# Spline chunks as single steps in the PSUM ring, and a new table of step offsets, in a transformer block of 16 sequences

## The reference

```python
x = x + _L0_attn_ref(_layernorm(x, axis=-1), L0_attn_wq, L0_attn_wk, L0_attn_wv, L0_attn_wo)
x = x + _L0_ffn_ref(_layernorm(x, axis=-1), L0_ffn_gate_cp, L0_ffn_up_cp, L0_ffn_down_cp)
# attention: 16 heads of 16; scores q.k / 4, masked where j - i > 16; softmax; times v; times wo.T
# ffn: the three weights are Catmull-Rom splines through about 2033 control points each:
gate_w = spline_reconstruct(gate_cp, INTER, HIDDEN)     # 1024 x 256
up_w = spline_reconstruct(up_cp, INTER, HIDDEN)
down_w = spline_reconstruct(down_cp, HIDDEN, INTER)     # 256 x 1024
inter = jax.nn.silu(gate) * up
return jnp.einsum('bsi,hi->bsh', inter, down_w)
```

## Time and profile before

| what | value |
|---|---|
| median of 3 runs | 655.34 us (653.92 to 655.53) |
| the profiled execution | 653.66 us |
| its span | 651.9 us |
| TensorE busy | 611.8 us (94%), 5568 matmul records |
| VectorE busy | 481.1 us (74%) |
| ScalarE, GpSimd busy | 267.9 us (41%), 200.5 us (31%) |

### The profile page before, as it was taken

One profiled execution on the slowest core, in us unless ns is written; L12 is line 12 of the kernel. 1 busy time (PEld: TensorE's weight loads), 2 busy tenths in 40 slices (PEclk: granted clock), 3 DMA queues, 4 the chain that ended last, 5 costly groups with the idle time before them and its releaser, 6 DMA issues.

```text
span 651.9 us, 14038 instructions
## 1 busy us (share of the span) xinstructions
PE 611.8 (94%) x5568; PEld 527.4 (81%) x5568; DVE 481.1 (74%) x935; ACT 267.9 (41%) x432; POOL 200.5 (31%) x244
## 2 busy tenths in 40 slices
PE   1878989999999999999999999999999999998977
PEld 0455547989889888989888988889898989887977
DVE  6776647876877888787879797878878796863442
ACT  2230345452444445354444345444534444444412
POOL 1540232332233232323332333323232332333313
PEclk9986779999999999999999999999999999998989
DMA  8133030302122322213040312222221303010000
GB/s 229 44 130 113 10 123 6 113 18 98 37 69 62 98 66 69 81 46 102 9 127 14 107 42 82 66 82 67 71 79 33 115 2 116 17 35 1 18 18 17
DMA packets 44113, 42.86 MB, mean 66 GB/s; under 512 B 4528, under 2 KB 42512, under 8 KB 44048
## 3 DMA queue, kind: packets, MB, share of 16 engines
q1 hardware_dynamic: 44048, 41.96, 20.7%
HBM read 12.32 MB, written 4.19 MB: 25 GB/s over the span
## 4 chain that ended last, share of the span: by engine, by line
PE 77%; DVE 19%; issue 2%; POOL 1%; ACT 0%; DVEq 0%; ACTq 0%; POOLq 0%
PE ring L605 13%; PE ring L606 11%; PE ring L607 11%; PE ring L689 6%; PE pair L657 6%; PE ring L612 5%; DVE M L547 5%; PE ring L614 5%; PE ring L613 5%; PE ring L596 4%; PE pair L681 3%; DVE Z L526 3%; PE pair L633 3%; DVE pair L541 2%; PE ring L696 2%
## 5 line engine op out<-in xcount | busy, mean ns | idle before, releaser
L605 PE MATMUL ring<-YT,WGUh 128*128 128x256 f32 x512 | 153.4, 300 | 0.1
L547 DVE TENSOR_REDUCE M<-pair 128x2 f32<-128x288 f32 (+1 forms) x256 | 134.7, 570 | 15.4 <-PE pair L666 11.7
L606 PE MATMUL ring<-YT,WGUh 128*128 128x256 f32 x512 | 144.9, 283 | 0.0
L607 PE MATMUL ring<-YT,WGUl 128*128 128x256 f32 x512 | 144.5, 282 | 0.0
L452 ACT ACTIVATE P<-pair 128x800 f32<-128x800 f32 x128 | 107.1, 838 | 87.5 <-PE pair L681 87.4
L410 POOL TENSOR_TENSOR IN<-GU,IN 128x512 fp32r<-128x512 f32 x64 | 82.2, 1284 | 161.0 <-ACT IN L415 161.0
L605 PEld LDWEIGHTS ring<-YT,WGUh 128*128 128x128 f32 x512 | 97.1, 190 | 6.8 <-issue 3.6
L606 PEld LDWEIGHTS ring<-YT,WGUh 128*128 128x128 f32 x512 | 97.3, 190 | 0.0
L607 PEld LDWEIGHTS ring<-YT,WGUl 128*128 128x128 f32 x512 | 96.9, 189 | 0.0
L402 POOL TENSOR_SCALAR_AFFINE_SELECT P<-P 128x448 f32<-128x448 f32 x64 | 37.6, 588 | 172.7 <-ACT P L452 172.7
L577 DVE SCALAR_TENSOR_TENSOR GU<-GU,ring 128x512 f32<-128x512 f32 x64 | 44.0, 688 | 61.1 <-ACT GU L473 61.0
(11 more groups left out here) (79 smaller groups left out, 1115.1 us busy)
## 6 DMA issues: line engine op xcount, KB each, us to landing
QM<-QK SPq DMA_DIRECT2D x96, 128.0 KB, 2.1
KS<-QK SPq DMA_DIRECT2D x96, 128.0 KB, 2.1
X<-x SPq DMA_DIRECT2D x32, 256.0 KB, 2.9
out<-X SPq DMA_DIRECT2D x16, 256.0 KB, 2.2
OVER<-over SPq DMA_DIRECT2D x4, 256.0 KB, 9.1
TAP<-points SPq DMA_DIRECT2D x4, 192.0 KB, 7.3
POWER<-powers SPq DMA_DIRECT2D x4, 192.0 KB, 7.6
P<-wqk SPq DMA_DIRECT2D x1, 512.0 KB, 5.5
```

The source lines that it names most:

```text
L547: i = nc.vector.tensor_reduce(out=M[:, t % 2, it, :].rearrange("p (a k) -> p a k", a=2)[:, :, n], in_=pr[:, :, cols], axis=AX.X, op=ALU.ma ...
L605: mm(o, wh[:, kb, c], act[:, 0, kb, :], start=j == 0 and kb == 0, stop=False, skip_group_check=True)
L606: mm(o, wh[:, kb, c], act[:, 1, kb, :], start=False, stop=False, skip_group_check=True)
L607: i = mm(o, wl[:, kb, c], act[:, 0, kb, :], start=False, stop=False, skip_group_check=True)
```

## The change

The chunk is no longer done in pairs. It becomes two steps, `wj` (part 0) and `ws` (part 1), each one matmul with a bank of its own in the ring of four; `s1` and `sc` have the two pairs of banks to themselves. VectorE multiplies after `wj` and adds after `ws`. The quarters of the weights are made in the order 0, 2, 1, 3 (`PIECES`), in which `ga` and `up` use them. Waits are cut into pieces: `qk`, `v` and `wo` wait for their own `raw_low`; `ga` and `up` of n = 0, 1 for four chunks in place of eight; `dn` for ten, then twelve. Two guards are added for memory that is used again (`tapped` before the first tanh, `ws_sum` before the first `ic`), and `OVER` and `POWER` change places in memory. All offsets and `PERIOD` are new; turn 3 gets a table of its own.

```diff
+PIECES = (0, 2, 1, 3)
-PERIOD = 33.072
+PERIOD = 33.644
-START = [("raw", 0, 1, 1, -101.93, 0), ("split", 0, 1, 1, -96.87, 0), ("tap", 0, 4, 1, -38.33, 3.572),
+START = [("split", 0, 1, 1, -659.307, 0), ("raw", 0, 1, 1, -233.876, 0), ("tap", 0, 4, 1, -227.012, 29.8767),
...
-RING = ("zt", "qk", "v", "mt", "av", "ot", "on", "wo", "z2", "ga", "up", "dn")
-PAIRS = ("s1", "sc", "ws")
+RING = ("wj", "ws", "zt", "qk", "v", "mt", "av", "ot", "on", "wo", "z2", "ga", "up", "dn")
+PAIRS = ("s1", "sc")
...
-            free[b] = at["y", t, 0] if what == "dn" else k
+            free[b] = at["y", t, 0] if what == "dn" else at["ws", t, n] if what == "wj" else k
...
+                    if t == 0 and n == 0:
+                        act.wait_ge(tapped, len(PIECES))
...
+                    if t == 0 and n == 0:
+                        act.wait_ge(ws_sum, CHUNKS)
...
-                    dve.wait_ge(ws_made, n + 1)
+                    dve.wait_ge(wj_made, n + 1)
                     if n >= 4:
                         dve.wait_ge(ws_low, n - 3)
-                    w, pr = shaped(W[:, n % 4, :], n), pair(what, t, n)
-                    tt(w, shaped(pr[:, 0, :], n), spline_over(n), ALU.mult).then_inc(ws_over, 1)
+                    w = shaped(W[:, n % 4, :], n)
+                    tt(w, shaped(bank("wj", t, n)[:], n), spline_over(n), ALU.mult).then_inc(ws_over, 1)
+                    dve.wait_ge(ws_made, n + 1)
                     dve.wait_ge(ws_over, n + 1)
-                    tt(w, w, shaped(pr[:, 1, :], n), ALU.add).then_inc(ws_sum, 1)
+                    tt(w, w, shaped(bank(what, t, n)[:], n), ALU.add).then_inc(ws_sum, 1)
...
-                elif what == "ws" and (n % 2 or n >= 8):
+                elif what in ("wj", "ws"):
+                    m, j = chunk(n)
+                    part = ("wj", "ws").index(what)
                     pe.wait_ge(rows_loaded, DMA)
...
+                    pe.wait_ge(tapped, PIECES.index(j) + 1)
+                    mm(bk[:], ROWS[32 * m:32 * m + 32, part, :], TAP[32 * m:32 * m + 32, j * 512:(j + 1) * 512],
+                       start=True, stop=True).then_inc((wj_made, ws_made)[part], 1)
...
-                    pe.wait_ge(raw_low, 3)
+                    pe.wait_ge(raw_low, 1)
...
-                    pe.wait_ge(ws_low, 8)
+                    pe.wait_ge(ws_low, 4 if n < 2 else 8)
...
-                    pe.wait_ge(ws_low, CHUNKS)
                     part, j = divmod(n, 2)
+                    pe.wait_ge(ws_low, CHUNKS - 2 + 2 * part)
```

More of the change, by code:

```diff
@@ L146, in steps_of_turn @@
 def steps_of_turn(t):
-    return steps(FIRST_TURNS[t] if t < len(FIRST_TURNS) else TURN)
+    return steps(OWN.get(t, TURN))
 def all_steps():
@@ L243, in build @@
             TAP = early.enter_context(nc.sbuf_tensor("TAP", [96, NQ], F32))
+            OVER = early.enter_context(nc.sbuf_tensor("OVER", [128, NQ], F32))
             POWER = early.enter_context(nc.sbuf_tensor("POWER", [96, NQ], F32))
-            OVER = early.enter_context(nc.sbuf_tensor("OVER", [128, NQ], F32))
             W = early.enter_context(nc.sbuf_tensor("W", [128, 4, 512], F32))
@@ L265, in build @@
             "wo_made", "z2_made"))
-        ga_made, up_made, dn_made, ws_made = map(sem, ("ga_made", "up_made", "dn_made", "ws_made"))
+        ga_made, up_made, dn_made, wj_made, ws_made = map(sem, ("ga_made", "up_made", "dn_made", "wj_made", "ws_made"))
         zt_high, qk_high, v_done, exp_done, av_done, on_high, z2_high, tanh_done, in_high = map(sem, (
@@ L287, in emptied @@
                     "wo": wo_done, "z2": z2_low, "ga": ga_done, "up": up_done, "sc": exp_done,
-                    "ws": ws_sum}[what]
+                    "wj": ws_over, "ws": ws_sum}[what]
             return done, nth(*step)
@@ L303, in chunk @@
         def chunk(u):
-            return (u % 2, u // 2) if u < 8 else (2, u - 8)
+            return (u % 2, PIECES[u // 2]) if u < 8 else (2, u - 8)
         def spline_part(u, part):
@@ L333, in _ @@
                     sp.dma_start(raw(0, 2), wqk.rearrange("(k p) c -> p k c", p=128)).then_inc(raw_loaded, DMA)
-                    for j in range(4):
+                    for j in PIECES:
                         c = slice(j * 512, (j + 1) * 512)
@@ L493, in _ @@
                 if what == "tap":
-                    dve.wait_ge(points_loaded[n], 3 * DMA)
-                    c = slice(n * 512, (n + 1) * 512)
+                    j = PIECES[n]
+                    dve.wait_ge(points_loaded[j], 3 * DMA)
+                    c = slice(j * 512, (j + 1) * 512)
                     tt(TAP[:, c], TAP[:, c], POWER[:, c], ALU.mult).then_inc(tapped, 1)
                 elif what == "ws":
-                    dve.wait_ge(ws_made, n + 1)
+                    dve.wait_ge(wj_made, n + 1)
                     if n >= 4:
                         dve.wait_ge(ws_low, n - 3)
-                    w, pr = shaped(W[:, n % 4, :], n), pair(what, t, n)
-                    tt(w, shaped(pr[:, 0, :], n), spline_over(n), ALU.mult).then_inc(ws_over, 1)
+                    w = shaped(W[:, n % 4, :], n)
+                    tt(w, shaped(bank("wj", t, n)[:], n), spline_over(n), ALU.mult).then_inc(ws_over, 1)
+                    dve.wait_ge(ws_made, n + 1)
                     dve.wait_ge(ws_over, n + 1)
-                    tt(w, w, shaped(pr[:, 1, :], n), ALU.add).then_inc(ws_sum, 1)
+                    tt(w, w, shaped(bank(what, t, n)[:], n), ALU.add).then_inc(ws_sum, 1)
                 elif what in ("la", "ma"):
@@ L623, in _ @@
                     pe.wait_ge(ident_loaded, DMA)
-                elif what == "ws" and (n % 2 or n >= 8):
+                elif what in ("wj", "ws"):
+                    m, j = chunk(n)
+                    part = ("wj", "ws").index(what)
                     pe.wait_ge(rows_loaded, DMA)
-                    pe.wait_ge(tapped, chunk(n)[1] + 1)
-                    us = (n - 1, n) if n < 8 else (n,)
-                    if n < 8 and BEFORE.get((what, t, n - 1)):
-                        pe.wait_ge(*emptied(BEFORE[what, t, n - 1]))
-                    for part in range(2):
-                        for u in us:
-                            m, j = chunk(u)
-                            i = mm(pair(what, t, u)[:, part, :], ROWS[32 * m:32 * m + 32, part, :],
-                                   TAP[32 * m:32 * m + 32, j * 512:(j + 1) * 512], start=True, stop=True)
-                            if part:
-                                i.then_inc(ws_made, 1)
+                    pe.wait_ge(tapped, PIECES.index(j) + 1)
+                    mm(bk[:], ROWS[32 * m:32 * m + 32, part, :], TAP[32 * m:32 * m + 32, j * 512:(j + 1) * 512],
+                       start=True, stop=True).then_inc((wj_made, ws_made)[part], 1)
                 elif what == "zt":
@@ L644, in _ @@
                 elif what == "v":
+                    pe.wait_ge(raw_low, 2)
                     pe.wait_ge(zt_low, nth("zt", t, 0))
@@ L701, in _ @@
                 elif what == "wo":
+                    pe.wait_ge(raw_low, 3)
                     pe.wait_ge(on_low, nth("on", t, 0))
```

6 lines of the change are left out of this document (2 added, 4 removed), and 87 rows, old and new, of tables (FIRST_TURNS, OWN, START, TURN).

## The result

The changed kernel took 633.63 us (median of 4 runs, 628.83 to 643.22) against 655.0 us of the kernel before (653.92 to 655.53): ratio 0.965, 95% interval 0.955 to 0.975. Four more runs in a later job gave 629.45 us (628.35 to 630.62), ratio 0.961, interval 0.959 to 0.963. Here and in the table further down, a ratio leaves out every run that was over 1.5% above the fastest of its kernel (643.22 here, two runs of experiment 10 there), so it is not the quotient of the two medians. Two of the first four (638.02 and 643.22 us) had a mean granted clock over the span of 0.970 and 0.963, the other six runs 0.986 to 0.989. The profiled run took 629.24 us (span 627.5), 24.4 us less than the profiled 653.66 of before.

The account below looks back on a forecast made before the run. TensorE, busy 94% of the span, was taken as the bound, with time to win in start, turn and tail: 653.66-6.5-1.8-2.9-8.0 = 634.5 us (636.1 against the median), predicted 635 us; own range 630 to 640, 8-in-10 range 624 to 646.

Parts of the forecast that it names:

- The start, 6.5 us: Before turn 0's first ga: earlier VectorE multiplies and new order bring that ga from 114.46 to 108 us, 6.5 us earlier.
- only a `ws` and the following `wj` can overlap: Spline chunks at the start: in the new order no other chunk matmuls overlap on TensorE; 3 units for four matmuls, against 2.
- 3 units: First two chunks: four matmuls take three units of about 1.9 us, 5.6 us in place of 3.79.
- rival A: Start: chunks cost no more TensorE time, or VectorE hides it; first ga at 101 us, total 627.5 us; chance 0.15.
- B: Start: every chunk runs alone at low clock, ring banks make TensorE wait; first ga 115.5 us, total 642 us; chance 0.24.
- The 2.5 us for the cold stretch: First sc to first ga: added to a full-clock walk of 42 us, because 71 to 106 us ran at 0.80 clock.
- Five more steps ahead of `ga`, 1.8 us: Start: sc and s1 of heads 0, two ot and one zt moved ahead of first ga, leaving 1.8 us less behind.
- The turn, 2.9 us: Repeating turn: more steps cover z2's wait for Z, removing a 0.32 us stall in 9 turns, 2.9 us.
- Rival C: Repeating turn: wo comes too early for OTT, waiting 1.55 us in 15 turns, 23 us; total 657.5 us; chance 0.04.
- The tail, 8.0 us: Turns 14 and 15: waits for Z of 1.83 and 3.29 us and the half clock after them go, 8.0 us.
- `wo` may now wait 0.2 us: Tail: with z2's waits for Z gone, wo itself may wait 0.2 us per turn.
- The waits by pieces, nothing: Start: cutting waits into pieces (raw_low, ws_low, tapped, ws_sum) costs and gives nothing, as all twelve chunks precede first ga.

Follow-up runs that it names:

- experiment 10: Changed kernel with two extra 128-row matmuls of 512 columns ahead of each matmul of chunks 3 to 7; 651.97 us.
- Experiment 6: Changed kernel with order wj n, wj n+1, ws n, ws n+1 for chunks 0-1, 4-5 and 6-7; 637.83 us.
- experiments 3: Changed kernel's order, but each chunk again one step with a pair of banks and one signal; 645.43 us.
- 7: Changed kernel, order and ring kept, but VectorE multiplies only once both matmuls of a chunk are done; 638.34 us.
- experiment 2: Kernel before with one dn put ahead of z2 and one behind it in turns 4 to 13; 652.69 us.
- experiment 4: Changed kernel with the waits put together again (raw_low 3, ws_low 8 and 12); 630.09 us.
- experiments 1: Kernel before with six dn steps of turns 13 and 14 moved; 649.51 us.
- 11: Kernel before with six dn steps of turns 13 and 14 moved, and their last ic moved behind the last up; 648.44 us.
- experiment 8: Experiment 6 with two extra 128-row matmuls of 512 columns ahead of each matmul of chunks 8 to 11; 640.74 us.
- experiment 9: Kernel before with two extra 128-row matmuls of 512 columns ahead of each matmul of chunks 8 to 11; 664.18 us.

## Why the prediction held, and where it did not

The forecast was 635.0 us. It got 633.63, with 629.24 in the profiled run; the sum against that run (634.5) was 5.3 us too high. That the median came within 1.4 us of the forecast is luck: it lies between two runs of 629 and two of 638 and 643 us that had a lower clock, no run took it, and the repeat's median was 629.45.

- **The start, 6.5 us.** Measured 8.7 us (114.46 to 105.73). Of its milestones, the first `sc` was forecast at 63.5 and stood at 63.6; the eight heads were to end at 55.7 and ended at 56.0. Others were off in ways that made up for each other: the fourth chunk matmul was done at 18.0, not 19.35, and the last `W` of chunk 7 at 42.0, not 40.0. The step that failed is "only a `ws` and the following `wj` can overlap", with its "3 units" for the first two chunks: the four matmuls took 4.01 us, 2.1 units of 1.9, for `wj` of the next chunk runs ahead of the `ws` that stands before it. For chunks 3 to 5 the count came out right in sum. Experiment 6 shows that the difference is worth nothing by itself: rival A's condition (no unit lost) was nearly met for the first two chunks, and the first `ga` stood at 105.7, not at 101; B's (all four lost) did not come. The sentence "By the rule alone the sum would be rival B's" also does not follow from the one ahead of it: a `ws` and the next `wj` read different row groups, so the rule gives 3 units, not B's 4.
- **The 2.5 us for the cold stretch.** This term is where the start was mis-sized. From the first `sc` to the first `ga` the sum had 42 + 2.5 = 44.5 us, and the changed kernel took 42.1: the 2.4 us between them are the whole of the 2.2 us by which the start was off. I took the half clock of the kernel before (0.80 from 71 to 106 us) as a surcharge on a walk at full clock; it ran at 0.95, with 3.4 us at half clock in that stretch, which can cost 1.7 us at most. The term could as well have been three times too small: the profiled runs of experiments 3, 6 and 7 took 50.3, 49.9 and 50.1 us for the same steps, 20.5 to 24.0 us of it at half clock. The prediction had no rival with this mechanism. It may be the largest part of the start: of the 8.7 us that the first `ga` gained, up to (27.3 - 13.7) / 2 = 6.8 us are clock. How much of it is clock was not shown apart. The two of eight runs of the changed kernel that took 9 and 14 us more had a lower mean clock; even the one at 0.970 is 17 us faster than the kernel before at 0.971 (655.19 us), so 17 of the 25.7 us do not hang on the mean clock.
- **Five more steps ahead of `ga`, 1.8 us.** Not measured apart. It lies in the 3.4 us that the stretch from the first `ga` to that of turn 5 became shorter, where the prediction had these 1.8 and some turns at 0.32.
- **The turn, 2.9 us.** The wait for `Z` is gone, no wait for VectorE's `OTT` came in the turns from 240 to 523 us, and a turn went from 35.47 to 35.10: 0.37 rather than 0.32, over 9 turns 3.3 us. Rival C (23 us of waits for `OTT`) did not happen; experiment 2 shows its like in small, a new wait of 0.24 us (1.9 us in 8 times) behind `zt` that took back most of the gain when only the cover was moved.
- **The tail, 8.0 us.** Confirmed in the main: 6.8 us by moving eight steps of the kernel before, and at most 0.9 of the 1.1 us of `OTT` waits that this left. Of my "`wo` may now wait 0.2 us" exactly one case came, in the waits from 560 us on:

```profile
PE ring L637 <- DVE OTT L510: 0.2, 1, 0.2
```

- **The waits by pieces, nothing.** Confirmed by experiment 4.
- **The rest.** The part behind turn 12's `ga` gave 9.6 us, against 8.0 and some turns at 0.32: the 5.3 us by which the sum was too high are 2.2 in the start and 3.0 spread behind it, each of them a term slightly too small.

## What to carry to other kernels

Walk the queues of a pipelined start with durations from the trace: here such a walk had the first `sc` right to 0.1 us, though milestones inside it were off by 1 to 2 us and made up for each other. Then ask in a separate line what the granted clock may do, since here the same steps took 42 to 50 us with it, and it differed between runs of one kernel. When a version comes out slower, compare runs at the same mean clock, and TensorE's busy time for the same number of matmuls, before blaming the order. To remove a stall, look first at whom the cover is taken from (experiment 2), and take the producers of a moved step along (experiments 1 and 11).

## What the runs showed of the hardware

- **The half clock of the start comes without idle time ahead of it.** In the profiled run of experiment 10 TensorE is busy for 29.00 of 29.00 us at a mean granted clock of 0.64. Adding 128-row matmuls raised the time at half clock in the profiled runs of all three kernels (by 3.4, 20.5 and 44.4 us); two other runs of experiment 8 and one of experiment 9 had a mean clock as high as the best without them, or higher.
- **Matmuls of different row groups start past one that waits for its row group.** `wj` of chunk 1 (rows 32 to 63) starts 0.26 us after that of chunk 0 (rows 0 to 31), with `ws` of chunk 0 between them in the order. The Trainium skill (TensorE: Matmul & The Clock Gate, Part 3: Packing small matmuls — row/col tiling) lets matmuls of different row groups overlap, but says that they keep the order of the program in start and end. The records differ from the second half of that, and they decide.
- **A granted clock of 1.00 can be the lack of a record.** A lone chunk at 21.16 us takes 3.75 us and one at 54.49 us takes 1.98, though the view prints a granted clock of 1.00 for both places. Chunk, stretch, and the timeline where the pace changes, in the changed kernel:

```profile
21.16 3.75 PE L654 MATMUL ring<-TAP,ROWS 32*128 32x512 f32 x4 [2.12 <-DVE TAP L520]
```

```profile
20.00:26.00 6.00, 4.83 (x9) 2.32 (x10) 3.45 (x5) 1.33 (x3) 2.02 (x2) 1.00 0.00 1
```

```profile
27.79 0.41 PE L631 MATMUL ring<-ZT,WQKh 128*128 128x256 f32 x1
28.00 0.41 PE L632 MATMUL ring<-ZT,WQKl 128*128 128x256 f32 x1
28.21 0.32 PE L630 MATMUL ring<-ZT,WQKh 128*128 128x256 f32 x1
28.37 0.28 PE L631 MATMUL ring<-ZT,WQKh 128*128 128x256 f32 x1
28.49 0.28 PE L632 MATMUL ring<-ZT,WQKl 128*128 128x256 f32 x1
```

Up to 28.21 us matmuls of 256 columns start every 0.21 us, and behind it every 0.12 us. The trace's records of the granted clock begin at 28.3 us (between 27.7 and 30.9 us in the fourteen traces), with full clock, so pace and records agree; for the time before there is no record, and the view prints 1.00. The 0.88 and, in the earlier trace rows, the 0.94 for 14 to 42 us are therefore too high, and the column of half clock in the table leaves that first part out. Where a clock row may lack records, the duration of a known instruction shows the pace.
